# Eight time lags on TensorE: fp32 in 32-row strips, four at a time, in place of split bf16

## The reference

```python
# block 1, on x
ctx    = causal_ema(x, tau_ctx)
gated  = x * sigmoid([x, ctx] @ Wg.T + bg)
mod    = 0.5 + sigmoid(gelu(x @ Wn1.T) @ Wn2.T + bn2)            # D = 32 scales
traces = [causal_ema(gated * mod[..., d], tau[d]) for d in 32]
temporal = sum_d traces[d] * softmax(blend)[d]
out = (gelu(x @ Wsoma.T) * sigmoid(temporal @ Wtemp.T)) @ Wout.T
x = x + layernorm(out)
# block 2, on the new x: attention with 16 heads of 8 channels, keys either from a
# list of 32 indices per token or dense with a bias, by row
x = x + attention(x) @ Wo.T
```

## Time and profile before

| what | value |
|---|---|
| median of 3 runs | 326.8 us |
| the profiled execution's own time | 326.89 us |
| its span in the trace | 325.0 us |
| instructions | 9974 |
| PE, DVE, POOL, ACT busy | 94%, 85%, 77%, 66% |
| granted TensorE clock over the span | 0.999 |
| front and first step | 0 to 39.42 us |
| six closing steps | 39.42 to 155.34 us, 19.3 each |
| passage to attention | 155.34 to 197.19 us |
| attention in its rhythm, and its end | 197.19 to 325.0 us |

### The profile page before, as it was taken

How to read it: one execution, slowest core, us unless ns; L and a number is a source line. 1 busy time by engine, 2 the same in 40 slices (tenths; PEclk the granted TensorE clock), 3 DMA queues, 4 the chain that set the end, 5 groups by cost and what they waited for, 6 DMA issues and landing times. The chain is left out here.

```text
span 325.0 us, 9974 instructions
## 1 busy us (share of the span) xinstructions
PE 306.1 (94%) x3314; PEld 207.0 (64%) x3324; DVE 274.6 (85%) x1449; ACT 215.2 (66%) x459; POOL 248.8 (77%) x300
## 2 busy tenths in 40 slices
PE   8898899999999999999887989999999999999995
PEld 2554464656566465555535667887887887887873
DVE  3888899878978886797879669999999999999972
ACT  5862256545655655457674678878778878778863
POOL 3173586778686885665855869999999999999990
PEclk9999999999999999999999999999999999999999
DMA  6700120050311305013530435564544364210011
GB/s 184 222 2 1 32 67 34 17 130 3 105 42 57 90 0 144 4 33 65 75 60 2 87 95 83 82 139 126 126 105 117 93 126 105 78 32 6 3 34 34
DMA packets 29154, 23.07 MB, mean 71 GB/s; under 512 B 2736, under 2 KB 27824, under 8 KB 29104
## 3 DMA queue, kind: packets, MB, share of 16 engines
q1 hardware_dynamic: 29104, 22.44, 29.3%
HBM read 7.75 MB, written 2.10 MB: 30 GB/s over the span
## 5 line engine op out<-in xcount | busy, mean ns | idle before, releaser
L1609 POOL TENSOR_TENSOR arena<-arena,neg_max 128x512 f32<-128x512 f32 x128 | 129.9, 1052 | 10.8 <-DVE neg_max L1451 10.7
L1451 DVE CUSTOM_DVE_ANT_0 arena<-ps,arena 128x128 f32<-128x128 f32 x512 | 113.9, 287 | 9.6 <-issue 5.1
L1093 ACT ACTIVATE arena<-ps 128x512 f32<-128x512 f32 x128 | 69.6, 596 | 10.2 <-PE ps L789 10.2
L789 PE MATMUL ps<-ident_sb,arena 128*128 128x128 f32 x512 | 68.2, 276 | 0.0
L789 PEld LDWEIGHTS ps<-ident_sb,arena 128*128 128x128 f32 x512 | 56.5, 141 | 6.9 <-POOL arena L1609 4.0
L1528 POOL TENSOR_TENSOR arena<-arena 128x448 f32<-128x448 f32 (+6 forms) x56 | 42.8, 764 | 23.2 <-DVE arena L1283 19.6
L1451 DVE DVE_READ_ACCUMULATOR2_ANT neg_max<- 128x1 f32 x512 | 42.6, 83 | 0.0
L805 PE MATMUL ps<-arena 128*32 128x128 f32 x1024 | 41.2, 279 | 0.0
L1515 POOL TENSOR_TENSOR arena<-decay_a,arena 128x192 f32<-128x192 f32 x32 | 19.5, 637 | 22.0 <-ACT arena L930 22.0
L805 PEld LDWEIGHTS ps<-arena 128*32 128x32 f32 x1024 | 24.1, 109 | 6.9 <-issue 0.3
L775 PE MATMUL ps<-arena 48*128 48x128 bf16 x512 | 25.4, 219 | 2.4 <-DVE neg_max L1451 2.3
(11 more groups left out here) (172 smaller groups left out, 575.4 us busy)
## 6 DMA issues: line engine op xcount, KB each, us to landing
arena<-q_parts SPq DMA_DIRECT2D x96, 64.0 KB
arena<-k_parts SPq DMA_DIRECT2D x96, 64.0 KB
arena<-in_x SPq DMA_DIRECT2D x16, 256.0 KB, 3.3
arena<-in_xt SPq DMA_DIRECT2D x8, 256.0 KB, 2.8
out<-arena SPq DMA_DIRECT2D x7, 256.0 KB, 3.0
arena<-in_consts SPq DMA_DIRECT2D x1, 420.0 KB, 3.8
w_sb<-in_w SPq DMA_DIRECT2D x1, 384.0 KB, 6.3
w_sb<-in_w SPq DMA_DIRECT2D x1, 192.0 KB, 4.1
```

The source lines that it names most:

```text
L789: mm = pe.transpose(ps[1][:, q % 2, k * P:k * P + P], neg_t[q % NT_RING][:, k * P:k * P + P], ident)
L1093: act.activation(probT[q % PT_RING], ps[1][:, q % 2, :], ACT.Exp, scale=-1.0)\
L1451: dve.tensor_tensor_reduce(out=neg_t[q % NT_RING][:, cs], in0=ps[0][:, score_bank(c) + slot, cs], in1=nbias[n % 2], scale=1.0, scalar=3.0e ...
L1609: pool.tensor_tensor(t4, t4, neg_max[:, n % 2, 4 * z:4 * z + 4].unsqueeze(2).broadcast_to([P, 4, P]), ALU.subtract).then_inc(s["shifted"], 1)
```

## The change

The bf16 parts go. The weights stay fp32 in `w_lag`, replicated over four 32-row strips as the modulation already is, and a quad of four lags runs as four fp32 matmuls of depth 32, one per strip, each into a bank of its own. Lags 0, 1, 6 and 7 use the group's own banks 0 and 1, lags 2 to 5 use banks 2 and 3 of the other set. `ctx` and `v` move to bank 3. The products get buffers for more lags at once (`prod`). The order of the steps changes on PE, ACT, DVE and POOL, with new waits where banks are shared; in the passage, scores and logits go ahead of the last groups' work.

```diff
-        lag_a = sb("lag_a", [P, Q, P], BF16)
-        lag_b = sb("lag_b", [P, Q, P], BF16)
...
+        w_lag_sb = sb("w_lag", [P, Q * P])
...
+        def lag_bank(m, lag):
+            return bank(m % 2, lag % 2) if lag in (0, 1, 6, 7) else bank(1 - m % 2, 2 + lag % 2)
...
+            def four_lags(i, m, first):
+                u = m % 2
+                if first == 0:
+                    pe.wait_ge(s["soma_ready"], grp(i, m, 1, 1))
+                    pe.wait_ge(s["modn_ready"], grp(i, m, 1, 1))
...
+                        pe.wait_ge(s["bh_ready"], grp(i, m, NJ + NCAR))
+                else:
+                    pe.wait_ge(s["prod_ready"], grp(i, m, Q, 4))
+                for lag in range(first, first + 4):
+                    rows_of = slice((lag - first) * D, (lag - first) * D + D)
+                    pe.matmul(lag_bank(m, lag), w_lag[rows_of, lag, :], thd[u][rows_of, :], start=True, stop=True)\
                         .then_inc(s["lag_ps"], 1)
...
# new waits on PE: f_context
-                    pe.wait_ge(s["modT_tanh"], grp(i, m, 1, 1))
+                    pe.wait_ge(s["centred"], grp(i, m, GB, -GB))
# b_gate, then b_out
+                    pe.wait_ge(s["prod_ready"], grp(i, m, Q, Q + 5))
+                    pe.wait_ge(s["prod_ready"], grp(i, m, Q, Q + 6))
...
# PE, closing step, new order behind f_context:
#   b_locals, f_soma(+1), f_modulation_n(+1), f_gate_ctx(+1), c_x1T(-1), four_lags(+1, 0), f_gated(+1),
#   b_cross, c_k, b_crossT, four_lags(+1, 4), c_less(k, 0), b_gate, c_q, c_less(k, 1),
#   b_out, c_less(q, 0), c_v, c_less(q, 1)
...
# DVE, closing step: b_carries, b_locals, f_gated, lags 0-3, b_temporal, lags 4-5, counts, b_mixed,
#   lags 6-7, counts, c_moments, c_centre, and in the last step neg_lc behind c_centre
-                    f_mod_parts(i, m + 1)
...
# ACT: f_mod_part1, f_mod_part1b, L996, L1003 removed; c_values and the Ln of the last step ahead of c_part(q, 2)
# POOL: lags 1-5, counted, lags 6-7, c_rstd, counted
...
# PE, front: four_lags(0), f_modulation(+1), f_gated, f_soma(+1), b_carries, four_lags(4), f_context(+1), f_gate_x(+1)
# DVE, front: lag_parts() and f_mod_parts() removed
# DVE, end():
-                b_mixed(LAST, 1)
                 logits(5)
+                b_mixed(LAST, 1)
-                c_moments(LAST, 1)
                 logits(6)
                 logits(7)
+                c_moments(LAST, 1)
# PE, end(): scores(3) ahead of b_out; PE, octets: scores(c + 3) ahead of the last group's c-phase;
# DVE, octet 1: logits(8), logits(9) ahead of c_residual(LAST, 1)
```

More of the change, by code:

```diff
@@ L174, in build @@
             gn.append(take(W))
-            prod.append([take(W), take(W)])
+            wide, temporal, two = take(W), take(W), take(W + P // 2)
+            third, fifth, sixth = 5 * W // 8, 3 * W // 8, 2 * W // 8
+            prod.append([None, wide, temporal, two[:, 0:third], two[:, third:], wide[:, 0:fifth],
+                         wide[:, fifth:fifth + sixth], temporal])
             modn.append(take(P))
-            weights_at = at[0] - 4 * W - P
         xn = [take(W) for _ in range(2)]
@@ L205, in build @@
         probT = [take(W) for _ in range(PT_RING)]
-        neg_t = [take(W) for _ in range(NT_RING - 2)] + xn
+        neg_t = [take(W) for _ in range(NT_RING - 2)]
+        neg_t[NT_RING - 3:NT_RING - 3] = xn
         yout = [take(W).rearrange("p (b c) -> p b c", b=GB) for _ in range(2)]
@@ L411, in _ @@
             for _ in range(12):
-                pe.matmul(bank(1, 3), mod_pb[0][:, 0:P], mod_pb[0][:], start=True, stop=True)
+                pe.matmul(bank(1, 3), zeros[:, 0:P], zeros[:, 0:W], start=True, stop=True)
             pe.wait_ge(s["small_loaded"], 32)
@@ L845, in octet_step @@
                     turn_o(n - 1)
+                if 1 <= c and c + 3 < 2 * B:
+                    scores(c + 3)
                 if c == 2:
@@ L855, in octet_step @@
                     c_v(LAST, 1)
-                if 1 <= c and c + 3 < 2 * B:
-                    scores(c + 3)
                 if c >= 1:
@@ L1385, in step @@
                 f_gated(i, m + 1)
-                f_lags(i, m + 1, range(0, 2))
+                f_lags(i, m + 1, range(0, 4))
+                if not closes:
+                    dve.wait_ge(s["const_ps"], 2)
+                    dve.wait_ge(s["rows_loaded"], 16)
+                    pro("kept_bias", dve.tensor_tensor(kept_bias[:], bank(1, 3)[:, 0:P], bo, ALU.add), waited=False)
+                b_temporal(i, m)
+                f_lags(i, m + 1, range(4, 6))
                 if first < last:
@@ L1487, in octet_step @@
                     logits(2 * c + 7)
+                if c == 1:
+                    c_residual(LAST, 1)
             pipeline(dve, front, step, end)
```

246 lines of the change are left out of this document (82 added, 164 removed).

## The result

The changed kernel takes 330.8 us (median of 7 runs, 329.72 to 332.58), the kernel before 327.28 beside it (7 runs, 326.6 to 330.15): ratio 1.0096, interval 1.0055 to 1.0137. It is slower by 1%, where 319.5 us, 2.2% faster, was forecast. The runs of the changed kernel differ by 2.9 us, the shortest with a mean granted clock of 0.990 and the longest with 0.978. Its profiled run took 330.5 us with a span of 328.7, against 325.0.

What follows compares the result with a forecast made beforehand. PE was taken to set the closing steps, largely by chains through DVE and ACT, and POOL the attention stretch. Scores 7.1 us earlier and passage -0.3 made -7.4 on the 325.0 span: 319.5 us, range 315 to 324.5.

Steps and rivals of the forecast that it cites:

- The quad: Four fp32 lag matmuls in four strips on PE: 1.0 us per quad, two taking 2.0 instead of 3.5.
- rival 3: A quad's four matmuls do not run together, up to 2.4 us more a quad: 354 us, 5%.
- Front: Work before the closing steps: `b_locals` of group 0 at 22.75, first closing step at 36.3 instead of 39.42, -3.1 us.
- The closing step, 18.4: Each ordinary closing step takes 18.4 us instead of 19.27, 0.9 less; the first 19.3, the last 19.0.
- five parts: Closing step cut at `b_locals`, first quad, `b_gate`, `b_out` and end: 4.1 + 3.8 + 5.75 + 2.5 + 2.25 us.
- PE's own issue time: Sum of PE's starts in a closing step, said to fall to about 17.4 us.
- rival 1: DVE's products become the bound, 0.2 us lost at each of four hand-offs, step 19.2: 324.3 us, 20%.
- The granted clock is 1.00 throughout: PE's clock taken as full over the whole run, with no cost put on it.
- The passage, -0.3: From first scores to POOL's unbroken run: POOL enters 0.3 us earlier relative to the first scores.
- Bias, residual and x1's turn at about 6.3: In the passage, x1's turn comes 6.3 us after the scores instead of 4.8, +1.5 on group 7's b-phase.
- +1.5 if only the delay stays: Upper bound on the passage's change, if no gains offset the later x1 turn; lower bound -2.4.
- Slower at 6%: Chance that the whole kernel gets slower, made up of rival 3 and some more.

Runs made afterwards that it cites:

- s2: s1 with the last four products also reading other banks, so `b_gate` and `b_out` no longer wait for lags 4 and 5: 326.66 us, one run.
- s1: Changed kernel without the second quad's matmuls (lags 4 to 7) for groups 2 to 7, waits kept: 328.72 us, one run.
- f1: Changed kernel with 26 more idle matmuls in the passage's three PE gaps and 14 in the first step (the filled kernel): 327.07 us, ratio 1.0001.
- f2: Kernel before without its 11 idle matmuls ahead of group 6's x1 turn: 330.09 us, ratio 1.0094.
- g2: f1 with the last group's moments ahead of logits 6 and 7 and its residual ahead of logits 8 and 9: 328.95 us, ratio 1.0054.
- h1: f1 with group 6's residual ahead of POOL's first bias sum, and 10 instead of 20 idle matmuls ahead of group 6's x1 turn: 326.01 us, ratio 0.9959.
- h3: h1 with the logarithm placed earlier on ACT, as in g3: 325.64 us, ratio 0.9953.
- h4: h3 with the last group's rstd behind the shifts of logits 6 and 7 on POOL: 324.87 us, ratio 0.9922.
- p1: Changed kernel with the passage's whole order put back as in the kernel before: 328.83 us, ratio 1.0046.
- g1: f1 with the passage's whole order put back as in the kernel before: 331.39 us, ratio 1.0118.
- g3: f1 with the logarithm ahead of the second q part and the values' copy on ACT: 327.17 us, ratio 1.0001.
- p2: Changed kernel with group 7's moments ahead of logits 6 and 7 and its residual ahead of logits 8 and 9: 330.58 us, ratio 1.0115.
- p3: Changed kernel with `neg_lc` ahead of `c_centre` on DVE and the logarithm behind q's last split on ACT: 331.43 us, ratio 1.0133.
- p4: Changed kernel with 26 more idle matmuls in the passage's three PE gaps: 327.94 us, ratio 1.0019.
- g4: f1 with the edits of g2 and g3 together: 329.01 us, ratio 1.0050.

## Why the prediction was wrong

- **The quad: right.** 1.0 us forecast, 1.08 to 1.19 measured. That the four matmuls run side by side (rival 3) is settled; its 34 us did not come.
- **Front: right.** `b_locals` of group 0 at 22.80 (forecast 22.75), first closing step at 36.80 (36.3). Of the way from one to the other, 14.0 us against 13.55, the four parts took 0.03 to 0.16 more each.
- **The closing step, 18.4: the step that failed first.** By its five parts, forecast then measured: 4.1, 4.13; 3.8, 3.97; 5.75, 6.05; 2.5, 2.58; 2.25, 2.47. The pauses at `b_gate` and `b_out` are where they were named (0.5 each forecast, 0.33 and 0.40 in the trace). What was sized wrong is PE's own issue time, put at 17.4. It came to about 18.1: 19.20 less the two pauses, which are 0.49 and 0.56 when counted from the start of the split before each, at 0.22 for a split. Up to the split behind the second quad the trace shows no wait of PE, and yet the second quad is 0.4 late (12.4 us into the step, 12.0 forecast). From start to start `b_locals` takes 1.06 instead of 0.95, `soma` behind it 1.06 instead of 0.86, the quads 1.19 and 1.08 instead of 1.0, and, each behind its pause, `b_gate` 0.94 instead of 0.86 and `b_out` 1.00 instead of 0.89. The prediction had 0.1, for `soma`, as the only change of tiling outside the quads. That a group costs more beside one of another height (32 rows beside 128) is argued from these places, not tested. 19.2 is the figure of rival 1, but by luck: its "0.2 lost at each hand-off" isn't where most of the time went. Only a part of rival 1's mechanism is there: s2, which frees `b_gate` and `b_out` of the wait for the products of lags 4 and 5, gains 0.46. And s1 shows that a shorter issue time of PE late in the step would have given little, 0.38 of 1.07. Four steps at 0.8, the last 0.3 and the first 1.3 (of which 0.5 are the clock: 20.63 against 20.13 in f1) are 4.8 us. The Trainium skill's rule (TensorEngine Tiling (Array Packing), PSUM Bottleneck), which the forecast set aside, is that emptying PSUM may become the bottleneck; the trace agrees with its outcome, a step 0.07 shorter, and with its mechanism by the 0.46 of s2.
- **"The granted clock is 1.00 throughout": true of the trace of before, wrong of what was forecast.** The prediction put pauses of PE down as time that PE does not need. This is the second step that failed: the filled kernel shows 3.3 us of span for their effect on the clock. The trace of before warned: the kernel issued 11 idle matmuls in the very place where its PE would wait (ten of them are in the trace, in the line below), and f2 shows that they are worth 3.5 us. The change kept their number and lengthened the wait behind them from 0.55 to 2.15 us. The Trainium skill (TensorE: Matmul & The Clock Gate, Loop structure matters more than you think) says that a long wait for DMA between matmuls lets the clock go down. The trace agrees, here with waits for POOL and DVE: 2.03 against 1.13 us for one group of matmuls.

```profile
157.28 2.32 PE L731 MATMUL ps<-mod_pa,lag_a 128*128 128x512 bf16 x10
```

- **The passage, -0.3: the third step, wrong in sign and size.** At full clock it was +2.5 (44.35 against 41.85). "Bias, residual and x1's turn at about 6.3" was right, 6.13, and was then netted against gains on other engines, which came out too small. They are not nothing: g2, which takes logits 6 to 9 back behind the moments and the residual, loses 1.9. But POOL, which sets the entry, stood in its own queue with finished work behind what it waited for. Three moves in the queues of ACT and POOL (h1, h3, h4) return 1.1, 0.4 and 0.8 us. The upper bound written down, "+1.5 if only the delay stays", was too low as well.
- **Slower at 6%.** The one mechanism named for that side was the quad in series. A pause of PE behind which the clock is halved was not among the rivals; it decides the sign, for f1 without it stands at 1.0001 (0.9984 to 1.0018), neither faster nor slower.

What stays open: h4 recovers 2.2 us against f1, but how much of the 2.5 us lies with each piece of the passage's new order isn't separated. The one run of p1 with a clock of 1.00, 326.32 us, hints that its old order is worth 0.75 against f1; g1, which was to show it, lost the clock. And what decides whether the clock falls behind a pause isn't shown; the table at the end has pauses of one length with either outcome.

## What to carry to other kernels

When a change takes work off PE, walk the step by the chain through the other engines first; PE's saved time is worth only what that chain leaves, and count each group of PE by the start of the next one in the new order, since a group beside one of another height took 0.1 to 0.2 us more here. Price every new pause of PE by the clock as well, and put idle matmuls in the pause, no more of them than it is long: behind it they may run at the lower clock (p1, g1), and beyond it they become the wait (g3). On an engine that runs its queue in order, look at what stands ready behind each instruction that waits; moving one such instruction gave 0.8 us, where the new lags gave 0.07 us in a step.

## What the runs showed that I had not expected

- A pause of PE and a lower clock behind it went together often, not always. Most low stretches are about 3 us long; some, as g1's (0.50 from 156 to 162) and p2's (0.50 from 177 to 183), are twice that. In the profiled runs:

| pause of PE, us | low clock behind it | clock stayed at 1.00 |
|---|---|---|
| 0.66 to 0.69, then 1.03, about 180 us | f2, p1 | kernel before |
| 1.46, ahead of group 1's first quad | p1, p3, p4, s1 | changed kernel, p2, s2 |
| 1.60, ahead of the first step's `b_out` | changed kernel, p3, p4, s2 | p1, p2, s1 |
| 1.72 to 1.99, ahead of scores 5 | p2, s2 | changed kernel, p3, s1, g2, g4 |
| 2.15 to 2.37, ahead of group 6's x1 turn | changed kernel, p2, s2 | s1 |
| 2.27 to 2.28, ahead of group 7's x1 turn | changed kernel, p3, s1 | |
| 2.60, ahead of group 7's carries | p1, g1 | p3 |
| 2.91, ahead of group 6's x1 turn | f2 | |

- The kernel before seems to have this in some of its own runs: of the 27 beside h1 to h4, 15 took 326.5 to 326.8 us at a mean granted clock of 0.996 to 1.00, nine 327.9 to 328.5 at 0.990 to 0.998, and three 327.19, 327.29 and 329.08 at 0.997, 0.997 and 0.994. The ranges of the clock overlap, and none of the long runs has a trace. f1's ten runs lie within 0.21 us of each other.
- The same residual of the last group, four 128x128 instructions on DVE, took 1.41 us in the kernel before and 2.76 in the changed one, where POOL subtracted maxima at the same time; 1.43 in g2, where POOL stood idle for most of it, as in the kernel before. The Trainium skill (SBUF — State Buffer, Who interferes with whom) says that a DVE instruction with two SBUF inputs contends with a GpSimd (POOL) instruction that reads SBUF. The traces agree: the changed kernel's residual runs from 178.06 beside POOL's maxima from 176.07 to 180.15.
